# Post-norm block and two windowed-attention layers on one core: two norms moved behind the low parts on VectorE, and the inverse sums' DMA moved on SyncE

## The reference

```python
h = shift_token(x)
q, k, v = split(h @ wqkv)            # 8 heads of 64
q = l2norm(q) * qs ; k = l2norm(k) * ksc
q, k = rotary_xpos(q, k)
o = local_attention(q, k, v)         # blocks of 128 queries see their own and the block before
x = x + o @ wo
h = layer_norm(shift_token(x)) ; a, g = split(h @ w1 + b1)
x = x + (a * gelu(g)) @ w2 + b2
```

## Time and profile before

| | |
|---|---|
| median of 3 runs | 1808.09 us |
| profiled execution, its own time | 1808.74 us |
| its span, first to last instruction | 1807.0 us |
| busy: TensorE, VectorE, ScalarE, GpSimd | 95%, 83%, 65%, 58% |
| mean granted TensorE clock | 0.991 |
| first attention B (its `scale_o`) | 590 to 982 us |
| second attention B | 1208 to 1600 us |

### The profile page before, as it was taken

How to read it: one execution, slowest core, us unless ns; L and a number is a source line. 1 busy time by engine, 2 the same in 40 slices (tenths; PEclk the granted TensorE clock), 3 DMA queues, 4 the chain that set the end, 5 groups by cost and what they waited for, 6 DMA issues and landing times.

```text
span 1807.0 us, 43288 instructions
## 1 busy us (share of the span) xinstructions
PE 1722.9 (95%) x15168; PEld 1475.8 (82%) x15168; DVE 1503.3 (83%) x3862; ACT 1170.2 (65%) x3024; POOL 1043.5 (58%) x996
## 2 busy tenths in 40 slices
PE   6999999999999999999997999989999999989997
PEld 5787777789997788888886888878888888878886
DVE  6888888868878889889896778799898898856776
ACT  6999888854445778777774343457777777733332
POOL 3676565533325677777763455366777767633343
PEclk9999999999999999999999999999999999999999
DMA  3111211032312222222213434232222222222221
GB/s 106 37 37 40 69 37 31 25 105 82 113 59 100 60 74 64 78 64 74 71 55 88 146 104 129 96 115 60 78 64 75 75 63 78 59 85 66 81 81 36
DMA packets 183075, 133.83 MB, mean 74 GB/s; under 512 B 21080, under 2 KB 182112, under 8 KB 182112
## 3 DMA queue, kind: packets, MB, share of 16 engines
q1 hardware_dynamic: 182880, 131.37, 23.8%
HBM read 92.52 MB, written 38.80 MB: 73 GB/s over the span
## 4 chain that ended last, share of the span: by engine, by line
PE 56%; DVE 30%; issue 8%; ACT 3%; DMA 2%; SPq 1%; DVEq 0%; POOL 0%; POOLq 0%; ACTq 0%
PE psum L594 14%; PE psum L596 13%; PE psum L595 13%; DVE masked L1354 7%; DVE g_in L1329 4%; PE psum L709 3%; PE psum L898 3%; PE psum L691 3%; DVE b_pt L1464 3%; DVE g_in L1300 2%; ACT a_probs L1733 2%; DVE g_in L1472 2%; PE psum L644 1%; DVE a_neg_max L1222 1%; DVE psum L1220 1%
## 5 line engine op out<-in xcount | busy, mean ns | idle before, releaser
L1852 ACT ACTIVATE b_probs<-masked,neg_max 128x256 f32<-128x256 f32 (+1 forms) x512 | 249.8, 490 | 125.9 <-DVE neg_max L1354 125.9
L594 PE MATMUL psum<-wa_hi,b_h_hi 128*128 128x512 f32 (+1 forms) x576 | 239.9, 416 | 19.1 <-DVE b_h_lo L1294 14.7
L1354 DVE CUSTOM_DVE_ANT_0 masked<-psum,mask 128x256 f32<-128x256 f32 (+1 forms) x512 | 177.3, 412 | 73.9 <-PE psum L898 73.9
L596 PE MATMUL psum<-wa_hi,b_h_lo 128*128 128x512 f32 (+1 forms) x576 | 215.2, 374 | 0.0
L595 PE MATMUL psum<-wa_lo,b_h_hi 128*128 128x512 f32 (+1 forms) x576 | 214.6, 373 | 0.0
L594 PE MATMUL psum<-g_h_hi,wm_hi 128*128 128x512 f32 (+1 forms) x480 | 190.4, 397 | 1.0 <-DVE y_out L1385 1.0
L2077 POOL TENSOR_TENSOR g_in<-g_in,minus_half 128x16 f32<-128x16 f32 x64 | 188.0, 2938 | 4.5 <-DVE g_in L1306 4.5
L596 PE MATMUL psum<-g_h_hi,wm_lo 128*128 128x512 f32 (+1 forms) x480 | 189.4, 395 | 0.0
L595 PE MATMUL psum<-g_h_lo,wm_hi 128*128 128x512 f32 (+1 forms) x480 | 189.3, 394 | 0.0
L1472 POOL TENSOR_TENSOR g_in<-g_z,g_in 128x512 f32<-128x512 f32 x62 | 79.9, 1289 | 163.7 <-DVE g_in L1300 158.5
L594 PE MATMUL psum<-wm_hi,u_hi 128*128 128x256 f32 x576 | 164.3, 285 | 0.1
(11 more groups left out here) (167 smaller groups left out, 5441.8 us busy)
## 6 DMA issues: line engine op xcount, KB each, us to landing
b_inv_t<-inverse_rows SPq DMA_DIRECT2D x128, 128.0 KB, 3.0
x_mid<-y_out SPq DMA_DIRECT2D x96, 128.0 KB, 1.8
rope_in<-in_rope SPq DMA_DIRECT2D x64, 128.0 KB, 2.3
x_res<-x_state SPq DMA_DIRECT2D x64, 128.0 KB, 2.3
g_in<-x_mid SPq DMA_DIRECT2D x32, 256.0 KB, 3.7
g_old<-x_state SPq DMA_DIRECT2D x16, 512.0 KB, 4.0
out_x<-g_fin SPq DMA_DIRECT2D x15, 512.0 KB, 2.9
w_raw<-in_w_mlp_b SPq DMA_DIRECT2D x2, 2154.0 KB, 9.0
```

The source lines that it names most:

```text
L594: nc.tensor.matmul(out, a_hi, b_hi, start=first, stop=False)
L596: return nc.tensor.matmul(out, a_lo, b_hi, start=False, stop=last)
L1354: ins = nc.vector.tensor_tensor_reduce(out[:, at], src[:, at], (mask if now else mask0)[:, at], -1.0, BIG, ALU.add, ALU.min, neg_max[:, r, ...
L1852: ins = nc.scalar.activation(out, src, ACT.Exp, bias=neg_max[:, r, k:k + 1], scale=-1.0, accum_out=row_sum[:, n % 2, 4 * r + k:4 * r + k + 1])
```

## The change

In the attentions B, the queries' and keys' norms of chunk s+2 stand behind `k_t_low` and `q_t_low` of chunk s+1 in VectorE's list, keys' first. On SyncE `store_inverse` stands at the head of each step, ahead of both parts of the MLP; chunk 0's store and spread are no longer behind `opening="last"`, and chunk 30's store is ahead of `opening=True` while its spread stays behind it. In the last step `invert_sums` stands ahead of the MLP's first normalization. In memory, `b_o` and `b_o_hi` lie where `b_inv_t` was, which lies further on now; `scale_o(0)` therefore waits for the zero row of the MLP ahead.

```diff
         row_sum = sbuf("row_sum", [P, 2, 8], at=b_ctx)
+        b_o = sbuf("b_o", [P, 512], at=b_ctx)
+        b_o_hi = sbuf("b_o_hi", [P, 512], F32R, b_ctx)
+        sbuf("b_gap", [P, 16], at=b_ctx)
         b_inv_t = sbuf("b_inv_t", [P, 2, 4, P], at=b_ctx)
-        b_o = sbuf("b_o", [P, 512], at=b_ctx)
-        b_o_hi, b_o_lo = sbuf("b_o_hi", [P, 512], F32R, b_ctx), sbuf("b_o_lo", [P, 512], F32R, b_ctx)
+        b_o_lo = sbuf("b_o_lo", [P, 512], F32R, b_ctx)
...
-        sbuf("b_space", [P, 1552], at=b_ctx)
+        sbuf("b_space", [P, 1544], at=b_ctx)
...
             for s in range(-1, B_LAST):
+                if b_chunk(s):
+                    store_inverse(s)
                 if s == NCH - 2:
                     sp_mlp(sp, MLP_B, MB, layer, opening=True)
-                if b_chunk(s) and s > 0:
-                    store_inverse(s)
+                if b_chunk(s):
                     spread_inverse(s)
...
                 if s == 0:
                     sp_mlp(sp, *mlp_behind(layer), None if layer == 0 else layer - 1, opening="last")
-                    store_inverse(0)
-                    spread_inverse(0)
...
             def scale_o(n):
...
                 v.wait_ge(S["pv_done"], 2 * (g0 + n) + 2)
+                if n == 0:
+                    v.wait_ge(zero_rows_stored, layer * 32 + 16)
...
                 if s == NCH - 1:
+                    invert_sums(s)
                     dve_mlp(v, MLP_B, MB, layer, opening=1)
-                    invert_sums(s)
...
                 if s == NCH - 2:
                     add_residual(s - 2)
-                if b_chunk(s + 2) and s + 2 > 1:
-                    norms(s + 2, 1)
                 if b_chunk(s):
                     copy_probs(s, 1)
-                if b_chunk(s + 2) and s + 2 > 1:
-                    norms(s + 2, 0)
...
                 if b_chunk(s + 1):
                     k_t_low(s + 1)
                     q_t_low(s + 1)
+                if b_chunk(s + 2) and s + 2 > 1:
+                    norms(s + 2, 1)
+                    norms(s + 2, 0)
```

## The result

The changed kernel takes 1925.46 us (median of 4 runs, 1924.39 to 1926.57) beside 1807.09 for the kernel before on the same chip: ratio 1.0652, 95% interval 1.0633 to 1.067. The profiled span is 1922.7 us, 115.7 longer than before.

What follows compares the result with a forecast made beforehand. The prediction had the present 12.67 us loop of TensorE and VectorE give way to a longer loop over GpSimd. Turns +111.2, layer starts +2.5 and ends -6.0 made +107.7 on 1808.7: 1916 us, range 1843 to 1940.

Steps and rivals of the forecast that it cites:

- The 29 turns of a layer: From `scale_rotated(2)` to `scale_rotated(31)`: 21 turns of 14.1 us and 8 with a piece of 15.8, 422.5 us together.
- The pieces: MLP low weights made on GpSimd between `o_low` and the power in eight steps a layer: turn 15.8 us, not 14.1.
- an allowance: For TensorE's clock falling in its idle time, or other lock orders: 0.4 us a turn, 23 us over 58 turns.
- the loop over GpSimd: Scaling, transposes, low parts, keys' norm, `rotate_k`, `o_low`, power, next scaling: 12.94 us without conflicts, 14.1 with them.
- each conflict as laid out: Rotation waits for `o_low` until 6.07 us, power ends at 9.57 instead of 8.97, scaling stands 0.65 behind the tables.
- several of its signs: GpSimd's power makes scalings wait around 1 us a chunk; pair 1.8 us, rotation product over 1.2; TensorE waits for scalings.
- the low parts then come sooner for TensorE: With two sums of about 0.64 us each and a clamp behind `q_t_low`, TensorE gets VectorE's low parts earlier.
- Taking turns in SBUF: VectorE and GpSimd exclude each other on SBUF: scalings 1.83 us instead of 1.28, GpSimd's rotation sum 2.15 instead of 1.25.
- The stores: Moved stores and sums at both ends of the two layers: +2.5 us at the starts, -6.0 at the ends.
- At the start: `scale_o(0)` waits for the zero row: +1.0 us in the first layer, +1.5 in the second; bounds 0 and +2 each.
- At the end: Chunk 30's earlier store shortens the wait of `scale_o(30)`: 3.0 us a layer, between 1.5 and 3.7, -6.0 in all.

Runs made afterwards that it cites:

- The two runs with one part each: Only the norms' move on the kernel before: 1925.92 us; the changed kernel with the norms back in their old places: 1810.18 us.
- 1875.09: Changed kernel with the keys' norm back ahead of the second probabilities copy, queries' norm and clamp between `q_t_low` and residual: 1875.09 us, turns 13.90.
- 1809.96: The kernel of 1875.09 with the clamp alone moved behind the residual: 1809.96 us, turns 12.73.
- 1925.92: The kernel before with nothing but the two norms moved behind `q_t_low`: 1925.92 us, ratio 1.0665.
- 1789.13: The kernel before, own stores and sums, with only the queries' norm and its clamp moved behind the residual: 1789.13 us, ratio 0.9898.
- 1788.55: Changed kernel with the keys' norm back ahead of `copy_probs(s, 1)`, queries' norm and clamp behind the residual: 1788.55 us, ratio 0.9906.

## Why the prediction was right, and where it wasn't

**Right: the size and the place.** 1916 was predicted and 1925.46 measured. The two runs with one part each show that the norms' move is all of it. The 29 turns of a layer were to come to 422.5 us and came to 425.2 and 424.4. That they came so close is in part luck. The pieces cost less than laid out (the term below), and TensorE's lower clock, for which the forecast itself had nothing and only the range an allowance, brought some 7 us a layer. The two nearly cancel.

**Half right: what binds.** The prediction closed one loop, over GpSimd. It is real: in the kernel with the residual first it binds with each conflict as laid out (rotation behind `o_low`, a longer power, scalings behind the tables), at 14.5 where 14.1 was worked out. Of the 0.4, 0.34 is the residual that this kernel puts ahead of the keys' norm. The further path of that kernel, by which the residual waits for TensorE, was not in the prediction either. But in the changed kernel itself the loop over GpSimd binds mainly where a piece of weights lies in it (15.9 to where the scaling gets going, predicted 15.8). The turn of 14.17 is a second loop, which the prediction left out: norm, norm, clamp, residual, scores, maxima, exponentials, copies, high and low parts. So several of its signs came only in turns with a piece, or not at all: the scalings' wait for the power is 2.7 us in 12 waits instead of 1 us a chunk, in the turn of 14.17 the pair takes 1.28 and not 1.8 and VectorE's rotation product 0.69 and not over 1.2, and the transposes' wait for the scalings is 30.1 us, not the main one. That both loops have nearly the same length, 14.17 and 14.1, is chance; the number was better than its reason.

**The step that failed** is the sentence that costs the norms at nothing else than GpSimd's lateness: "the low parts then come sooner for TensorE". What was queued behind the moved instructions, `add_residual`, and who waits for it, the scores, was not asked. With that wait taken away by putting the residual first, the order is slower still (1966.65): the residual's lateness had kept the two engines out of each other's way, and the residual ahead of the keys' norm waits for TensorE in its turn. What the second loop costs without the first, and with one norm in it, is shown by 1875.09, and that three quarters of its length over 12.33 come from the clamp's place (1.17 of 1.57 us a turn) by 1809.96.

**Taking turns in SBUF.** The prediction had it for the pair of scalings, the sums and the rotation, and it held where the engines meet. It left out the clamp. The rows of the clamp are the measurement: 0.17 us with GpSimd idle, 0.84 beside a GpSimd product over 512 columns and 1.15 beside such a sum, each time until that one has ended, while the norm (0.68 beside a GpSimd product over 512 columns at 906.42) and the residual (0.42 beside the sum at 903.17 in the kernel of 1809.96) pass. The Trainium skill ("SBUF — State Buffer", the section "Who interferes with whom") lists just that: a single-source op such as `tensor_scalar` can enter a mode that needs both ports and then blocks against GpSimd, a `tensor_reduce` on this chip never does, and neither does an op with at most one input in SBUF outside those modes. The trace agrees for all three.

**The pieces.** Predicted at 1.7 us for each turn with one. In the changed kernel a pair of turns, one with a piece, takes 15.36 + 13.99 = 29.35 where the clock stays at 1.00, so a piece costs 1.0 over two turns of 14.17, because the second loop's slack takes part of it. Where the loop over GpSimd binds it is 43 us for 16 pieces, 2.7 each, with what TensorE's lower clock and the residual's waits add.

**The stores.** -3.5 was predicted. The runs give +2.7 with the norms in their old places, -0.5 between 1925.92 and 1925.46 and -0.6 between 1789.13 and 1788.55, these two not clear of noise. At the start +2.5 was predicted and +2.9 measured. For `scale_o(0)` in the first layer it was 591.0 predicted and 590.91 measured, from the zero row's wait:

```profile
590.91 0.69 DVE L1381 TENSOR_TENSOR b_o<-psum,b_inv_t 128x512 f32<-128x512 f32 x1 [3.49 <-DMA x_state_sh<-zero_row]
```

That this is exact is chance: the zero row was issued at 589.72, 0.7 later than worked out, and landed 1.2 us after its issue, not 2.0. (The working also has 1.3 us for the spread, whose row has 2.28.) At the end -6.0 was mis-sized. The wait of `scale_o(30)` for the spread fell from 3.69 us to 2.05 in the first layer and from 3.87 to 2.43 in the second, not to under 1:

```profile
1030.89 0.69 DVE L1381 TENSOR_TENSOR b_o<-psum,b_inv_t 128x512 f32<-128x512 f32 x1 [2.05 <-DMA b_inv_t<-inverse_rows]
```

The spread still stands behind the MLP's loads, as the diff has it; half of the gain counted on was not there, and the end gives 2.9 us in all, 1.5 a layer, the lower bound of that term. How the rest divides between the spread's issue and its landing was not tried.

## What to carry to other kernels

When an instruction is moved to a later place in an engine's list, price two things: who waits for it, and who waits for each instruction that now stands behind it. A wait for a bank or a buffer, not for a value, is easily missed, since it shows no time as long as it is met. Where two loops are nearly as long, undoing one can make the kernel slower, by moving work into a conflict that its wait had kept apart; so take away each alone, from a version in which the other is open.

## What the hardware showed that was not expected

- A clamp over 128x16 took 0.17 us with GpSimd idle (554.29 in the kernel before) and 0.77 to 1.15 us when it started early in GpSimd's product or sum over 128x512. It ends 0.03 to 0.04 us behind the GpSimd instruction that it started beside, in every one of these kernels: 874.09 and 874.05 before, 907.71 and 907.68 in the changed one, 903.25 and 903.21 with turns of 13.90, 904.48 and 904.44 with turns of 12.73. Its length is thus set by when it starts, and moving it by one instruction was worth 65 us in 58 turns.
- The same holds the other way round: a power of 2.90 us took 3.36 when a rotation product of VectorE, which had stood behind `o_low`, ran as it began (the residual first), and GpSimd's tables 1.17 instead of 0.73 between the two scalings (the pieces behind the power).
- Two scalings of VectorE (1.28 us) took 1.81 when GpSimd's tables started with them, and 2.94 when a piece of weights of 1.32 us and then the tables did. A GpSimd instruction off every path costs what it holds up.
- Short idle times of TensorE came with a lower clock in some turns: between 672 and 676 us of the changed kernel, behind its wait of 1.95 us for the residual, the granted clock was 0.67 in the mean, so part of that stretch ran at the lower of the chip's two levels of 1.2 and 2.4 GHz, against 1.00 in the middle of the kernel before:

```profile
672.00:676.00 4.00, 4.00 (x49) 3.60 (x45) 3.68 (x17) 2.18 (x9) 4.00 (x4) 0.67 0.41 118
```

Of 17 waits of 1.95 us or a little more in the first layer 7 brought such a fall and 10 did not (the one that ended at 908.18 did not, and the stretch from 900 to 915 us has 1.00), and the kernel with turns of 13.90 ran at 1.00 between 660 and 860 us, with waits of up to 1.7 us ahead of the scores. What tells the turns apart was not tried.
